# A fused cross-product and attention block on one core: the prologue reordered, with its block sums split over three engines

## What is computed

```python
# x: (4, 512, 512), ctx: (4, 512, 512); FP8 with one scale per 1x128 (x) and per 128x128 block (ctx)
xq = quant_dequant_act_1x128(layernorm(x))
wq = quant_dequant_weight_128x128(ctx)
x = x + tanh(g_xattn[0]) * einsum('emk,enk->emn', xq, wq)
# causal attention, 16 heads of 32 (24 standard and 8 low-rank columns of Wa, scaled by sqrt of w_std, w_rec;
# low-rank parts of q and k swapped where w_rec > 0.1)
fused = layernorm(x) @ (Wa * col_scale)
y = softmax(causal(Q @ K.T / sqrt(32))) @ V
x = x + tanh(g_ffn[0]) * y @ Wp
```

## Time and profile before

| | us |
|---|---|
| median of 3 runs | 499.98 (499.82 to 503.68) |
| profiled execution | 499.74 |
| its span, first to last instruction | 497.9 |
| busy: PE, DVE, ACT, POOL | 440.6, 340.3, 255.7, 151.1 |

### The profile page before, as it was taken

How to read it: one execution, slowest core, us unless ns; L and a number is a source line. 1 busy time by engine, 2 the same in 40 slices (tenths; PEclk the granted TensorE clock), 3 DMA queues, 4 the chain that set the end, 5 groups by cost and what they waited for, 6 DMA issues and landing times.

```text
span 497.9 us, 7913 instructions
## 1 busy us (share of the span) xinstructions
PE 440.6 (88%) x2536; PEld 317.1 (64%) x2536; DVE 340.3 (68%) x1122; ACT 255.7 (51%) x498; POOL 151.1 (30%) x278
## 2 busy tenths in 40 slices
...
GB/s 225 197 1 87 39 246 82 91 69 96 146 2 2 89 101 193 67 56 95 141 27 0 64 97 127 138 53 98 97 11 2 58 102 97 64 95 102 60 21 86
DMA packets 27929, 42.62 MB, mean 86 GB/s; under 512 B 8272, under 2 KB 8528, under 8 KB 27888
## 3 DMA queue, kind: packets, MB, share of 16 engines
...
q0 software_dynamic: 192, 0.39, 0.3%
...
## 4 chain that ended last, share of the span: by engine, by line
PE 66%; DVE 24%; ACT 3%; issue 3%; DMA 2%; POOL 1%; SPq 0%; ACTq 0%; DVEq 0%; POOLq 0%
PE pv_bank L748 13%; DVE x_all L1201 10%; PE mm_bank L594 9%; PE mm_bank L595 8%; PE mm_bank L596 8%; PE exp_bank L734 6%; PE max_bank L717 5%; DVE max_bank L1230 5%; PE mm_bank L775 2%; PE mm_bank L777 2%; PE mm_bank L776 2%; PE turn_bank L610 2%; DVE bn L1208 2%; PE pv_bank L757 1%; DMA x_all<-in_x 1%
## 5 line engine op out<-in xcount | busy, mean ns | idle before, releaser
L1230 DVE CUSTOM_DVE_ANT_0 max_bank<-max_bank,causal 128x512 f32<-128x512 f32 (+3 forms) x256 | 121.0, 512 | 52.5 <-PE max_bank L717 52.0
L1002 ACT ACTIVATE work<-exp_bank 128x512 f32<-128x512 f32 (+1 forms) x192 | 94.9, 526 | 56.2 <-PE exp_bank L734 55.2
L512 POOL TENSOR_SCALAR_AFFINE_SELECT work<-work 128x384 f32<-128x384 f32 x64 | 33.4, 522 | 281.6 <-ACT work L1002 281.6
L748 PE MATMUL pv_bank<-work,v_aug 128*33 128x256 f32 (+3 forms) x512 | 78.9, 451 | 0.6 <-DVE work L1241 0.2
L734 PE MATMUL exp_bank<-q_stack,k_stack 97*128 97x512 f32 (+3 forms) x256 | 71.2, 341 | 7.6 <-ACT work L1002 6.5
L717 PE MATMUL max_bank<-k_stack,q_stack 96*128 96x512 f32 (+3 forms) x256 | 71.1, 338 | 2.4 <-DVE row_max L1230 1.8
L1201 DVE SCALAR_TENSOR_TENSOR x_all<-mm_bank,coef,x_all 128x128 f32<-128x128 f32 x224 | 61.5, 342 | 0.3
L748 PEld LDWEIGHTS pv_bank<-work,v_aug 128*33 128x33 f32 x512 | 29.7, 113 | 50.1 <-issue 42.1
L734 PEld LDWEIGHTS exp_bank<-q_stack,k_stack 97*128 97x128 f32 x256 | 45.6, 188 | 23.4 <-ACT work L1002 14.7
L594 PE MATMUL mm_bank<-xt_hi,w_hi 128*128 128x512 f32 x128 | 53.4, 417 | 0.7 <-ACT v_aug L981 0.7
L717 PEld LDWEIGHTS max_bank<-k_stack,q_stack 96*128 96x128 f32 x256 | 45.2, 191 | 12.7 <-DVE row_max L1230 3.7
...
## 6 DMA issues: line engine op xcount, KB each, us to landing
q_stack<-qk_hi SPq DMA_DIRECT2D x128, 64.0 KB, 2.0
...
```

The source lines that it names most:

```text
L512: pool.affine_select(out=three, in_=three, compare_op=ALU.is_ge, fill=0.0, base=0, pattern=[[0, 3], [1, P]], channel_multiplier=-1)
L748: last = pe.matmul(pv_bank[64 * j:64 * j + D + 1, P * m:T], v_aug[:, m, 2 * u + j, :], prob[j][:, PROB_COL[m]:PROB_COL[m] + T - P * m], st ...
L1002: act.activation(prob[j][:, UNIT_COL[k]:UNIT_COL[k] + UNIT_LEN[k]], exp_bank[(3 * j + k) % 2][:, 0:UNIT_LEN[k]], ACT.Exp, scale=SCALE).the ...
L1230: last = dve.tensor_tensor_reduce(max_bank[unit % 2][:, col:col + width], max_bank[unit % 2][:, col:col + width], causal[:, T - width:T], ...
```

## The change

- ctx(0) is loaded ahead of x(0), and its maxima and scales stand first. The inverse scales are released for POOL before the last multiply; the other factor takes tanh of the gate there (`ctx_scales`), behind a wait for the tanh. The coefficients become one product of two tensors (`coefficients`), for two tiles in a batch and for all four in the prologue.
- The scales of x are made for two tiles at a time (`G`, after two `F`).
- DVE copies the four turned ctx tiles out of PSUM (`f` in its list), which ACT did.
- Block sums of the first batch: of each tile DVE adds three, ACT multiplies the fourth by its coefficients (`s`) and POOL adds the product (`a`).
- The first six score tiles are made straight from the high and low parts, three matmuls of 32 rows each (`first_scores`), and don't wait for the stack.
- `first_x` lies in `v_aug`, whose ones are set later (POOL `v0`); the last quarter of Wa comes in three pieces, the last behind a wait for `j0`. The eight small loads for the column roots move from ACT's queue to SP's, behind Wa; three others on ACT now come after its sign tiles.
- All lists are new, in the prologue and in the batches. Semaphore counts follow.

```diff
-    "K3 max0 max1 S0 S1 max2 max3 S2 S3 S4 norm max4 max5",
-    "b0 S5 max0 S6 S7 max1 b1 max2 S8 max3 max4 S9 norm max5",
-    "S10 max0 max1 S11 t0 S12 max2 max3 H0 S13 max4 S14 b2 S15 t1 t2 max5 t3 norm b3 H1",
-    "A0 max0 max1 max2 max3 max4 max5 H2 norm",
...
+    "max0 max1 S0 S1 max2 max3 S2 max4 S3 S4 max5 S5 S6 norm",
+    "max0 S7 max1 b0 max2 S8 b1 max3 norm max4 max5 S9",
+    "S10 S11 max0 max1 t0 b2 max2 t1 S12 t2 S13 max3 S14 t3 H0 max4 max5 S15 norm b3 A0",
+    "max0 max1 H1 max2 max3 H2 max4 max5 norm A1",
...
-PE_FIRST = ("f0 f1 f2 f3 f4 S0 S1 S2 S3 f5 S4 S5 S6 f6 S7 S8 f7 S9 f8 S10 S11 S12 S13 S14 "
-     "S15 f9 f10 v0 f11 v1 q0 B0 B1 k0 V2 q1 M0 k1 M1 M2")
-ACT_FIRST = ("a0 C0 C1 C2 f0 d0 f1 C3 f2 C4 b0 f3 f4 C5 C6 f5 a1 C7 f6 b1 f7 N0 f8 a2 "
-     "a3 N1 f9 N2 b2 f10 N3 b3 v0 f11 v1 q0 k0 c0 V2 D0 c1 p0 q1 D1 k1 c2 c3")
-DVE_FIRST = ("x0 w0 x1 x2 x3 t0 t1 L0 L1 t2 t3 L2 A0 A1 T0 F0 F1 L3 F2 F3 T1 T2 c0 S0 "
-     "S1 S2 S3 b0 S4 S5 S6 S7 S8 b1 S9 S10 S11 S12 b2 S13 h0 S14 S15 b3 T3 h1 u0 u1 "
-     "h2 u2 h3 u3 B0 q0 B1 k0 M0 q1 M1 M2 k1")
-POOL_FIRST = ("i0 s0 s1 s2 s3 s4 s5 o0 s6 j0 s7 r0 j1 l0 l1 r1 l2 l3 r2 r3 j2 j3 g0 g1 "
-     "D0 g2 D1 g3 p0")
...
+PE_FIRST = ("f0 f1 f2 f3 f4 f5 S0 S1 S2 S3 S4 S5 f6 S6 S7 S8 S9 S10 S11 f7 S12 f8 S13 f9 "
+     "S14 S15 v0 v1.0 f10 v1.1 f11 v1.23 q0.0 B0 q0.123 B1 k0 V2 M0 M1 q1.01 M2 M3 q1.2 M4 q1.3 k1.012 M5 "
+     "k1.3")
+ACT_FIRST = ("d0 C0 a0 C1 a1 C2 C3 C4 C5 f4 b0 C6 f5 b1 s0 a2 f6 s1 C7 s2 a3 f7 N0 N1 "
+     "b2 f8 e3 f9 b3 s3 v0 N2 N3 f10 f11 q0 v1 p0 k0 c0 V2 c1 D0 D1 q1 c2 k1 c3")
+DVE_FIRST = ("t0 t1 t2 t3 A0 A1 x0 x1 w0 x2 x3 T0 L0 L1 F0 F1 G0 L2 L3 f0 F2 F3 f1 f2 "
+     "G1 f3 T1 c0 T2 T3 S0 S1 S2 S4 S5 S6 b0 b1 S8 S9 S10 S12 h0 S13 S14 b2 b3 h1 "
+     "u0 u1 u2 h2 h3 u3 B0 B1 q0 k0 M0 M1 M2 M3 M4 q1 M5 k1")
+POOL_FIRST = ("s0 s1 i0 l0 s2 s3 s4 s5 s6 s7 l1 j0 a0 j1 a1 r0 r1 l2 l3 a2 j2 a3 r2 r3 "
+     "o0 j3 g0 g1 g2 g3 D0 v0 D1 p0")
...
+            load_ctx(0)
             load_tiles(0, 0)
-            load_ctx(0)
...
+                elif kind == "a":
+                    pool.wait_ge(s_fmul, i + 1)
+                    pool.wait_ge(s_summed, 3 * i + 3)
+                    pool.tensor_tensor(x_tile(0, i), x_tile(0, i), tile_buf[:, i, :], ALU.add).then_inc(s_fadd, 1)
...
+            def first_scores(unit):
+
+                j, k = unit // 3, unit % 3
+                if unit == 0:
+                    pe.wait_ge(s_const, 3)
+                    pe.wait_ge(s_summed, 12)
+                    pe.wait_ge(s_fmul, NT)
+                    pe.wait_ge(s_qklo, 2)
+                if unit >= 2:
+                    pe.wait_ge(s_max, unit - 1)
+                rows = slice(D * j, D * j + D)
+                for i, col in MAX_UNITS[k]:
+                    width = P * (i + 1)
+                    dst, cols = max_bank[unit % 2][:, col:col + width], slice(P * i, P * i + P)
+                    pe.matmul(dst, qk_hi[rows, 0, 0, cols], qk_hi[rows, 0, 1, 0:width], start=True, stop=False)
+                    pe.matmul(dst, qk_lo[rows, 0, 0, cols], qk_hi[rows, 0, 1, 0:width], start=False, stop=False)
+                    last = pe.matmul(dst, qk_hi[rows, 0, 0, cols], qk_lo[rows, 0, 1, 0:width], start=False, stop=True)
+                last.then_inc(s_sm, 1)
...
+            def first_product(i):
+                act.wait_ge(s_coef, 1)
+                act.wait_ge(s_turn, i + 1)
+                act.wait_ge(s_cross, NK * i + NK)
+                for t in range(NT):
+                    last = act.activation(tile_buf[:, i, P * t:P * t + P], sum_bank(True, i, NK - 1)[:, P * t:P * t + P],
+                                          ACT.Copy, scale=coef[:, i, t, NK - 1:NK])
+                last.then_inc(s_fmul, 1)
...
-                scales(bank[:, 0:NT * NK], w_up[:], w_down[:], W_EPS).then_inc(s_wscale, 1)
+                chain(dve.tensor_scalar(w_down[:], bank[:, 0:NT * NK], W_EPS, None, ALU.max))
+                chain(dve.reciprocal(w_up[:], w_down[:]))
+                dve.tensor_scalar(w_up[:], w_up[:], FP8_MAX, None, ALU.mult).then_inc(s_wscale, 1)
+                dve.wait_ge(s_tanh, 1)
+                dve.tensor_scalar(w_down[:], w_down[:], gates[:, 0:1], 1.0 / FP8_MAX, ALU.mult, ALU.mult)
...
-                for i in range(lo, hi):
-                    last = dve.scalar_tensor_tensor(coef[:, i, :, :],
-                                                    x_down[:, i, :].unsqueeze(1).broadcast_to([P, NT, NK]), gates[:, 0:1],
-                                                    w_down[:].rearrange("p (n k) -> p n k", k=NK), ALU.mult, ALU.mult)
-                return last
+                w = w_down[:].rearrange("p (n k) -> p n k", k=NK)
+                shape = [P, hi - lo, NT, NK]
+                return dve.tensor_tensor(coef[:, lo:hi, :, :], x_down[:, lo:hi, :].unsqueeze(2).broadcast_to(shape),
+                                         w.unsqueeze(1).broadcast_to(shape), ALU.mult)
...
+            def first_scales(pair):
+                two = slice(2 * pair, 2 * pair + 2)
+                scales(x_amax[:, two, :], x_up[:, two, :], x_down[:, two, :], ACT_EPS).then_inc(s_xscale, 1)
...
+            def first_ctx(p):
+                dve.wait_ge(s_turn, p + 1)
+                dve.tensor_copy(wt_hi[:, :, P * p:P * p + P],
+                                first_bank(p)[:].rearrange("p (k c) -> p k c", k=NK)).then_inc(s_fctx, 1)
```

More of the change, by code:

```diff
@@ L138 @@
     "ACT": "copy z3",
-    "DVE": "z2 Z1 Z2 norm Z3 z3 Z8 Z9 Z10 Z11",
+    "DVE": "z2 Z2 norm Z3 z3 Z8 Z9 Z10 Z11",
 }
@@ L253, in flamingo_block @@
                  .rearrange("p (q h e) -> p q h e", q=2, h=H) for i in range(NK)]
-        late_raw = qk_hi[:].bitcast(FP32).rearrange("p g w t -> p (g w t)")[:, 0:NF]
-        raw_w = [work[:, 0:NF], work[:, NF:2 * NF], work[:, 2 * NF:3 * NF], late_raw]
+        V0, LOW0 = 2 * H * DS, 2 * H * DS + C
+        raw_w = [work[:, 0:NF], work[:, NF:2 * NF], work[:, 2 * NF:3 * NF]]
+        raw_qk = [raw[:, 0:V0] for raw in raw_w] + [raw_w[0][:, 0:V0]]
+        raw_v = [raw[:, V0:LOW0] for raw in raw_w] + [x_all[:, 1, 2, :]]
+        raw_low = [raw[:, LOW0:NF] for raw in raw_w] + [spare[:, 0:NF - LOW0]]
         raw_wp = y[:]
-        first_x = qk_lo[:].bitcast(FP32).rearrange("p g w t -> p (g w) t")
+        first_x = v_aug[:].rearrange("p i h e -> p i (h e)")[:, :, 0:C]
         w_amax = sb("w_amax", [P, NT * NK])
@@ L520, in weight_lo @@
             def weight_lo(k):
-                raw, tail = raw_w[k], tails[k]
-                v0 = 2 * H * DS
                 pool.wait_ge(s_wtailhi, k + 1)
@@ L711, in scores_for_max @@
                         pe.wait_ge(s_pstack[s], 48)
-                if unit >= 2 or not first:
-                    pe.wait_ge(s_max, 48 * n + 6 * u + unit - 1)
+                pe.wait_ge(s_max, 48 * n + 6 * u + unit - 1)
                 bank = max_bank[unit % 2]
@@ L829, in first_turn @@
                     turn_parts(first_x[:, i, :] if kind == "X" else tile_buf[:, i, :], first_bank(p))
-            for kind, i in pieces(PE_FIRST, True, True):
+            for kind, i, ks in parts_of(PE_FIRST, True, True):
                 if kind == "f":
@@ L850, in _ @@
                 elif kind == "M":
-                    if i == 0:
-                        pe.wait_ge(s_const, 3)
-                        pe.wait_ge(s_summed, 16)
-                    for unit in (2 * i, 2 * i + 1):
-                        scores_for_max(0, 0, unit // 3, unit % 3, first=True)
+                    first_scores(i)
                 else:
                     w = "qk".index(kind)
-                    if i == 0:
-                        pe.wait_ge(s_tlo, NT)
-                        pe.wait_ge(s_summed, 16)
-                        pe.wait_ge(s_wlo, NK)
-                    elif w == 0:
-                        pe.wait_ge(s_vcopy, 3)
-                    else:
-                        pe.wait_ge(s_qklo, 2)
-                    qk_product(w, i)
+                    if ks[0] == 0:
+                        if i == 0:
+                            pe.wait_ge(s_tlo, NT)
+                            pe.wait_ge(s_summed, 12)
+                            pe.wait_ge(s_wlo, NK)
+                        elif w == 0:
+                            pe.wait_ge(s_vcopy, 3)
+                        else:
+                            pe.wait_ge(s_qklo, 2)
+                    qk_product(w, i, ks)
             def body(b, more, ctx_more):
@@ L1042, in _ @@
                     weight_hi(i)
+                elif kind == "e":
+                    act.wait_ge(s_wqk, 16)
+                    weight_hi_qk(i)
                 elif kind == "b":
@@ L1191, in add_sum @@
                 at = NK * i + k
+                done = 3 * i + k if first else 16 * n - NT + at
                 dve.wait_ge(s_cross, 16 * n + at + 1)
@@ L1195, in add_sum @@
                 else:
-                    dve.wait_ge(s_sum, 48 * n + 3 * at)
+                    dve.wait_ge(s_sum, 3 * done)
```

(2 more changed lines are left out.)

143 lines of the change are left out of this document (82 added, 61 removed), and 83 rows, old and new, of tables (ACT_LAST, ACT_STEPS, DVE_LAST, DVE_STEPS).

## The result

The changed kernel takes 503.08 us, the kernel before beside it 500.76: ratio 1.0035, 95% interval [1.0022, 1.0049]. So it is slower by about a third of a per cent. I had predicted 499.0 with a range of 493 to 503; the time lies just above the range, on the side to which I gave little. The kernel before took 499.98 in the runs that the forecast started from and 500.76 here. Set against that, the top of the range would be near 504 and the time inside it; what is wrong without doubt is the direction, 1.0 us faster forecast and 2.3 slower measured.

A forecast was written before the change was run, and what follows sets the result against it. DVE bounds the prologue and the batches' block sums, PE the stretches between; DVE operations held by POOL add a price. First exponentials 0.2 us early plus 0.6 from the batches, 0.8 off 499.74, gives 498.9, by median 499.0; range 493 to 503.

The forecast's parts named there:

- The start: Prologue up to the first block sum: scaling s0 starts at 11.5 us, first sum at 35.3, against 31.68 before.
- rival (3): Prologue: gate loads land late, at 14 to 15, sliding x's statistics and first sum by 2.5 to 3 us; 502, chance 0.10.
- Rival (1): Prologue: DVE is held less, first sum at 29.1 to 31.2, 4.1 to 6.2 us earlier; 493 to 495, chance 0.26.
- the hold: DVE operations on SBUF alone that start inside a POOL instruction end just after it; put nine copies and c0 at risk.
- Block sums: First batch's sums: split over DVE, ACT and POOL worth 1.5 us at r3, not 4.1; q0 at 60.3, 0.6 late.
- T: Start time of the first block sum in the prologue, forecast at 35.3 us; q0 was to start 25.0 us after it.
- q0 to the exponentials: From q0 to the first exponential unit: 23.2 us against 24.0 before, a gain of 0.8.
- ACT ends this part: Between q0 and the first exponentials: ACT's chain of casts and copies sets the end, 23.2 us after q0.
- Batches: All four batches after the prologue: 0.6 us gained in all, bounds -3 and +1.
- Where PE is full, orders change only waits below 0.1 us: Batch stretches with TensorE full: new instruction orders were to change only waits under 0.1 us.
- Rival (2): Batches: new orders spare PE its idle 3.1 us and the lower clock behind it; 495, chance 0.09.
- Rival (4): Batches: one new order stalls a step of each of three batches by about 2 us; 505, chance 0.07.

The follow-up runs named there:

- b_waits: Kernel before, with one wait added: GpSimd's first low part j0 waits until the coefficients are done; 499.89 us, ratio 0.9983 to the kernel before.
- a_pool_waits: Changed kernel, with GpSimd's l1 (and j0 behind it) waiting until DVE's weight tails T1 to T3 are done; 500.83 us, ratio 0.9997 to the kernel before.
- a_one_product: Changed kernel, with each score for the first unit's maxima made by one product instead of three; 500.10 us, ratio 0.9976 to the kernel before.

## Why the prediction was wrong, step by step

The forecast's sum was 498.9; the profiled execution took 501.5 and 1.8 around it, 503.3. The 4.4 us between are these terms; between the medians, each against the kernel before beside it, the miss is about 3.3. In the start and the block sums the mechanism was right and the size too small; between q0 and the exponentials it had the wrong engine in front, and in the batches the reasoning itself failed.

**The start, +1.6.** s0 began at 12.07 (forecast 11.5), the last ctx tile landing at 9.1. The later gate load took 8.8 us and landed at 11.85, past the 11.3 I allowed but short of the 12.5 from which rival (3) decides; the gate multiply was held to 13.14. G1 ended at 28.83 (26.8 to 27.9), the first sum came 8.05 behind it (7.9): 36.88 against 35.3. Other executions with this start gave 35.15, 35.85 and 36.13, so the four average 36.0: about 0.7 of the 1.6 is a term too small, and the rest this execution. The structure was right: L0 and L1 held by l0 and s2 to 21.1 (20.5), T1 to T3 held by POOL's instructions one by one. The coefficient product came into a gap and took 0.21, and the copies out of PSUM were free, 0.68 each. Rival (1), less hold, was wrong, and b_waits and a_pool_waits show the hold itself, not the argument alone. It was in the sum from the start, and it is also the largest single cost found: without it after G1 the kernel is 1.9 us faster.

The Trainium skill, SBUF — State Buffer, section SBUF: two separate sides, says that the two engines' shared port pair, for the VectorE instructions that need it, is an exclusive lock for a whole instruction, the other fully blocking, not a bandwidth that is split. The runs agree: 0.30 us alone, 1.91 beside an instruction of 1.86. Which mode the held instructions run in no trace shows.

**Block sums, +0.7.** q0 came at T + 25.7 (25.0). I took 1.04 for POOL's add from its product; it took 1.27, four times, 0.9 in all. The split's 1.5 us at r3 was mis-sized, 0.7; that it was worth nowhere near DVE's 4.1 us, since POOL's queue sets q0, was right.

**q0 to the exponentials, +0.95.** 24.15 against 23.2. k1 was done 19.5 us behind q0 and not 18.0. The scores, matmuls of 32 rows, took 4.1 us (1.66, 0.90, 1.00 and 0.55 in the timeline) against 3.5: 0.23 per 512 columns as taken, plus about 0.1 at each change of operand, which also fell on every group of q1 and k1 between them. The order of the chain behind it was as written, but it took 4.6 us from k1 to the exponentials and not 5.2, so 0.95 of the 1.5 is left. "ACT ends this part" was wrong too, and by my own sum: there c2 ended at 17.5 and k1 at 18.0, so that ACT waited for TensorE. In the trace it waits 1.12 us for k1, and a_one_product shows TensorE's work to be on the path.

**Batches, +1.15.** +0.54 instead of -0.6, inside the bounds of -3 and +1. "Where PE is full, orders change only waits below 0.1 us" was the wrong step: the last batch, with TensorE 94% busy, gained 1.2 us (its busy time fell from 71.25 to 70.66 and its idle time from 4.5 to 3.9), and the first lost 1.6. The argument that DVE is full in the sums whatever the order was right (99% busy) and not enough. Rival (2), less low clock, went the other way. Rival (4), a stall of 2 us in each of three batches, did not come; the step that lost most was 0.75 longer (14.11 against 13.36). Of the first batch's 1.6 us the clock explains about 0.9 at most (a_one_product's first period, with 3.4 us of low clock, is 115.40); the rest is not taken apart.

**The chances.** 0.69 on no change by the 1% bound was right as far as it goes: 0.35% is within it, though that says nothing for the sum, which had the sign wrong. All four terms erred to one side, and each by less than I would have called an error. My range ended 4 us above the forecast because (4) was left out as a whole. The slow side lacked the case that came: several estimated durations a little too short.
